# A decoder layer: attention scores from the turned raw residual times a centred Gram matrix of the context, the second norm folded into the epsilon of the scores' norm

## What is computed

```python
x = x + L0_attn_ref(layernorm(x), Wv, Wg, bg, Wq, bq, Wo)
x = x + L0_xattn_ref(layernorm(x), ctx_512, W_k, b_k, gamma, beta)
x = x + L0_ffn_ref(layernorm(x), router_w, gate_w, up_w, down_w, ...)

def L0_xattn_ref(p, k_v, W_k, b_k, ln_gamma, ln_beta):
    kv = k_v @ W_k.T + b_k
    out = einsum('bij,bjd->bid', p, kv)
    sim = einsum('bid,bjd->bij', out, kv) * 256 ** -0.5
    sim = (sim - mean(sim)) * rsqrt(var(sim) + 1e-6) * ln_gamma + ln_beta
    return softmax(sim)
```

## Time and profile before

| what | value |
|---|---|
| time, three runs | 166.57 us median (164.66 to 167.26) |
| span of the profiled execution, first to last instruction | 155.8 us |
| PE busy | 119.9 us (77%) |
| DVE busy | 108.1 us (69%) |
| POOL busy | 101.7 us (65%) |
| ACT busy | 69.8 us (45%) |
| DMA, mean over the span | 112 GB/s |

### The profile page before, as it was taken

One profiled execution on the slowest core, in us unless ns is written; L12 is line 12 of the kernel. 1 busy time (PEld: TensorE's weight loads), 2 busy tenths in 40 slices (PEclk: granted clock), 3 DMA queues, 4 the chain that ended last, 5 costly groups with the idle time before them and its releaser, 6 DMA issues. The chain is left out here.

```text
span 155.8 us, 2769 instructions
## 1 busy us (share of the span) xinstructions
PE 119.9 (77%) x709; PEld 97.2 (62%) x710; DVE 108.1 (69%) x303; ACT 69.8 (45%) x164; POOL 101.7 (65%) x145
## 2 busy tenths in 40 slices
PE   0199997997599658669879794459999979999700
PEld 0158986993387338347659594327878859888500
DVE  2672596949897999999699977122676866776510
ACT  3445878494396726794344401011434333343100
POOL 5346695696588828967858578605377776777540
PEclk9999999999999999975899999965999999999975
DMA  5997465236222251440222258283243334111000
GB/s 141 229 279 211 157 184 157 68 83 192 65 52 85 71 135 23 120 126 0 74 70 69 103 203 299 84 268 103 77 113 104 117 101 148 50 58 44 31 0 0
DMA packets 18206, 17.51 MB, mean 112 GB/s; under 512 B 4108, under 2 KB 17424, under 8 KB 18192
## 3 DMA queue, kind: packets, MB, share of 16 engines
q1 hardware_dynamic: 15792, 13.56, 30.8%
q0 software_dynamic: 1824, 3.22, 6.5%
q10 hardware_dynamic: 576, 0.56, 1.1%
HBM read 13.78 MB, written 5.38 MB: 123 GB/s over the span
## 5 line engine op out<-in xcount | busy, mean ns | idle before, releaser
L437 POOL TENSOR_TENSOR gu_lo<-stage,gu_hi 128x512 fp32r<-128x512 f32 x16 | 22.4, 1410 | 2.8 <-ACT gu_hi L502 2.8
L452 POOL DMA_INDIRECT tq<-base_rows,tid x15 | 15.4, 1026 | 13.1 <-DMA base_rows<-res 6.2
L457 POOL DMA_INDIRECT out_dram<-z,tid x15 | 15.2, 1012 | 7.6 <-DVE tid L851 2.6
L478 ACT ACTIVATE xn<-res,shift,rstd 128x256 f32<-128x256 f32 x22 | 12.0, 593 | 8.2 <-POOL shift L413 8.1
L405 POOL TENSOR_SCALAR vareps<-mv 128x2 f32<-128x2 f32 x16 | 4.2, 259 | 15.7 <-DVE mv L673 15.0
L409 POOL TENSOR_TENSOR rstd<-vareps,expo 128x2 f32<-128x2 f32 x16 | 12.4, 772 | 0.4
L1057 PE MATMUL bV<-shd,xn 128*128 128x256 f32 x32 | 9.6, 453 | 2.0 <-DVE xn L818 2.0
L670 DVE BATCH_NORM_STATS2 bn<-res 128x6 f32<-128x256 f32 x24 | 8.9, 413 | 3.0 <-DMA res<-in_x_dram 3.0
L437 POOL TENSOR_TENSOR dn_lo<-stage,dn_hi 128x512 fp32r<-128x512 f32 x8 | 11.0, 1371 | 0.0
L432 POOL DMA_INDIRECT x_sorted<-xs,dest x8 | 8.2, 1031 | 4.0 <-issue 2.6
L982 PE MATMUL bO<-wo,tq 128*128 128x256 f32 x32 | 7.8, 386 | 3.8 <-issue 2.8
(11 more groups left out here) (200 smaller groups left out, 386.4 us busy)
## 6 DMA issues: line engine op xcount, KB each, us to landing
stage<-in_L_ffn_gate_w_dram SPq DMA_DIRECT2D x8, 256.0 KB, 2.8
stage<-in_L_ffn_up_w_dram SPq DMA_DIRECT2D x8, 256.0 KB, 2.7
stage<-in_L_ffn_down_w_dram SPq DMA_DIRECT2D x8, 256.0 KB, 2.7
xs<-x_sorted SPq DMA_DIRECT2D x15, 136.0 KB, 2.2
res<-in_x_dram SPq DMA_DIRECT2D x4, 256.0 KB, 3.5
base_rows<-res SPq DMA_DIRECT2D x4, 256.0 KB
x_sorted<-pad SPq DMA_DIRECT2D x5, 136.0 KB, 3.4
x_sorted<-pad ACTq DMA_DIRECT2D x4, 136.0 KB, 3.3
```

The lines of the kernel that those rows point to most:

```text
L437: g.tensor_tensor(units[n][2], stage[:, n % RING], f32(units[n][1]), ALU.subtract).then_inc(unit_lo, 1)
L452: g.indirect_dma_start(rb[:, s % TILE_RING, :], None, base_rows, bass.IndirectOffsetOnAxis(tid[:, s:s + 1], 0), bounds_check=N - 1, oob_is ...
L457: g.indirect_dma_start(out_rows, bass.IndirectOffsetOnAxis(tid[:, s:s + 1], 0), ry[:, s % 2, :], None, bounds_check=N - 1, oob_is_err=Fals ...
L478: last = a.activation(dst[:, i, :], res[:, b * TB + i, :], ACT.Identity, bias=shift[:, kind, b, i:i + 1], scale=rstd[:, kind, b, i:i + 1])
```

## The change

- `norm2`, `rstd2` and their tile `xn2` are gone. PE turns the raw residual (`turn2` waits for `x2_made`).
- `turn_kv`, `context_mix` and `mixed` are gone. Instead the context is centred once: `kv_bias` now also sums each row (two instructions for each half, with an accumulator), and DVE subtracts the mean (`centre_kv:0`, `centre_kv:1`). PE makes one Gram matrix per batch from it (`gram:b`, 256 by 256), and ACT copies each out (`gram_copy:b`).
- `similarity` is the turned residual times the Gram matrix: four products with a full contraction, in place of two with 64 rows.
- `sim_stats` is gone from DVE: the rows are centred already, so ACT takes the mean square from `bS` (`sim_square`, two `Square` with an accumulator) and POOL adds `eps_row`, which is the second norm's variance times the scores' epsilon (`sim_eps`, one instruction in the place of `rstd2`).
- `sim_centre` multiplies by `rstd` and gamma and so waits for `sim_rstd`; `sim_scale` only adds beta.

```diff
 DVE_ORDER
-    stats1:0 weight_lo:0 norm1:0 weight_lo:1 stats1:1 weight_lo:2 turned1_lo:0 stats1:2 stats1:3
+    stats1:0 weight_lo:0 norm1:0 weight_lo:1 stats1:1 weight_lo:2 turned1_lo:0 centre_kv:0 centre_kv:1
...
 ACT_ORDER
-    weight_hi:10 turned_kv:0 weight_hi:11 norm2:0 gate_tanh:2 query_tanh:2 weight_hi:12 turned2:0
+    weight_hi:10 gram_copy:0 gram_copy:1 gram_copy:2 gram_copy:3 weight_hi:11 gate_tanh:2 query_tanh:2
...
 PE_ORDER
-    turn1:2 recall:0 value:1 turn_kv:0 gate:2 query:2 value:2 turn2:0 recall:1 context_mix:0 turn1:3
+    turn1:2 recall:0 value:1 gram:0 gram:1 gram:2 gram:3 gate:2 query:2 value:2 turn2:0 recall:1 turn1:3
...
+            def sim_eps(b):
+                pool.wait_ge(stats[LN2], b + 1)
+                g.tensor_scalar(eps_row[:, b, :], mv[:, LN2, b, :, 1], SIM_EPS / SIM_SCALE ** 2, LN_EPS * SIM_EPS / SIM_SCALE ** 2,
+                                ALU.mult, ALU.add).then_inc(eps_row_made, 1)
...
+                if kind == SIM:
+                    pool.wait_ge(eps_row_made, b + 1)
+                    g.tensor_tensor(vareps[:, kind, b, :], spread[:, b, :], eps_row[:, b, :], ALU.add).then_inc(eps_added[kind], 1)
...
-                a.activation(kvT_all[:, 2 * h:2 * h + 2, :], (psU, psM)[h][0:C], ACT.Identity,
-                             bias=bk[:, :]).then_inc(kvT_made[h], 1)
...
+                for i in range(2):
+                    last = a.activation(kvT(2 * h + i), (psU, psM)[h][0:C, i, :], ACT.Identity, bias=bk[:, :],
+                                        accum_out=kv_sum[:, 2 * h + i:2 * h + i + 1])
+                last.then_inc(kvT_made[h], 1)
+
+            def gram_copy(b):
+                act.wait_ge(gram_done, b + 1)
+                a.copy(gram_all[:, b], (psS, psU, psM, psS)[b]).then_inc(gram_made, 1)
+
+            def sim_square(b):
+                act.wait_ge(sm["sim_done"], b + 1)
+                if b >= 1:
+                    act.wait_ge(stats[SIM], b)
+                for i in range(TB):
+                    last = a.activation(junk[:, i, :], psS[:, i, :], ACT.Square, scale=SIM_SCALE, accum_out=spread[:, b, i:i + 1])
+                last.then_inc(stats[SIM], 1)
...
+            def centre_kv(h):
+                dve.wait_ge(kvT_made[h], 1)
+                v.tensor_scalar(kv_mean[:, 2 * h:2 * h + 2], kv_sum[:, 2 * h:2 * h + 2], 1.0 / S, None, ALU.mult).then_inc(kv_mean_made, 1)
+                dve.wait_ge(kv_mean_made, h + 1)
+                for c in (2 * h, 2 * h + 1):
+                    last = v.tensor_scalar(kvT(c), kvT(c), kv_mean[:, c:c + 1], None, ALU.subtract)
+                last.then_inc(kv_centred[h], 1)
...
-                dve.wait_ge(stats[SIM], b + 1)
-                for i in range(TB):
-                    last = v.scalar_tensor_tensor(z[:, i, :], psS[:, i, :], mv[:, SIM, b, i, 0:1], gam[:, :],
-                                                  ALU.subtract, ALU.mult)
+                dve.wait_ge(rstd_made[SIM], b + 1)
+                for i in range(TB):
+                    last = v.scalar_tensor_tensor(z[:, i, :], psS[:, i, :], rstd[:, SIM, b, i:i + 1], gam[:, :],
+                                                  ALU.mult, ALU.mult)
...
+            def gram(b):
+                pe.wait_ge(kv_centred[b // 2], 1)
...
+                if b == 3:
+                    pe.wait_ge(gram_made, 1)
+                for m in range(KT):
+                    last = T.matmul((psS, psU, psM, psS)[b][:, m, :], kvT(b)[:, m * P:(m + 1) * P], kvT(b), start=True, stop=True)
+                last.then_inc(gram_done, 1)
...
             def similarity(b):
+                pe.wait_ge(gram_made, B)
                 pe.wait_ge(sm["xT2_made"], b + 1)
...
                 for i in range(TB):
+                    for k in range(KT):
+                        last = T.matmul(psS[:, i, :], xT2[:, b % 2, k, i * P:(i + 1) * P], gram_all[:, b, k, :],
+                                        start=(k == 0), stop=(k == KT - 1))
```

More of the change, by code:

```diff
@@ L54 @@
[L54 to L57, removed]
+    weight_hi:10 gram_copy:0 gram_copy:1 gram_copy:2 gram_copy:3 weight_hi:11 gate_tanh:2 query_tanh:2
+    weight_hi:12 turned2:0 norm1:3 weight_hi:13 sim_square:0 turned1_hi:3 weight_hi:14 weight_hi:15
@@ L66 @@
-    sim_scale:3 route:1 residual3:3 turned3_lo:2 shared_hidden:1 route:2 shared_add:0 destination:1
-    turned3_lo:3 destination:2 shared_hidden:2 route:3 shared_add:1 destination:3 slot_table:3
-    shared_add:2 shared_hidden:3 shared_add:3
+    stats1:0 weight_lo:0 norm1:0 weight_lo:1 stats1:1 weight_lo:2 turned1_lo:0 centre_kv:0 centre_kv:1
+    stats1:2 stats1:3 turned1_lo:1 memory:0 turned1_lo:2 residual2:0 memory:1 memory:2 residual2:1
+    turned1_lo:3 sim_centre:0 sim_scale:0 residual2:2 residual3:0 sim_centre:1 memory:3 sim_scale:1
@@ L69 @@
+    turned3_lo:0 residual2:3 sim_centre:2 residual3:1 sim_scale:2 shared_hidden:0 route:0 residual3:2
+    destination:0 turned3_lo:1 sim_centre:3 sim_scale:3 route:1 residual3:3 turned3_lo:2 shared_hidden:1
+    route:2 shared_add:0 destination:1 turned3_lo:3 destination:2 shared_hidden:2 route:3 shared_add:1
+    destination:3 slot_table:3 shared_add:2 shared_hidden:3 shared_add:3
 """.split()
@@ L487, in norm1 @@
                 normalise(LN1, b, xn1[:, b % 2], "xn1_made")
[L489 to L492, removed]
             def norm3(b):
@@ L596, in shared_tanh @@
                 a.activation(hs[:, b % 2], psG, ACT.Tanh, scale=0.5).then_inc(sm["th_made"], 1)
-            steps = {"norm1": norm1, "norm2": norm2, "norm3": norm3, "weight_hi": weight_hi, "turned_wk": turned_wk, "turned_ctx": turned_ctx, "kv_bias": kv_bias,
-                     "turned_kv": turned_kv, "mixed": mixed, "turned1_hi": turned1_hi, "gate_tanh": gate_tanh,
+            steps = {"norm1": norm1, "norm3": norm3, "weight_hi": weight_hi, "turned_wk": turned_wk, "turned_ctx": turned_ctx, "kv_bias": kv_bias,
+                     "gram_copy": gram_copy, "sim_square": sim_square, "turned1_hi": turned1_hi, "gate_tanh": gate_tanh,
                      "query_tanh": query_tanh, "turned2": turned2, "softmax_exp": softmax_exp,
@@ L831, in _ @@
             steps = {"stats1": stats1, "norm1": norm1, "weight_lo": weight_lo, "turned1_lo": turned1_lo,
-                     "memory": memory, "residual2": residual2, "sim_stats": sim_stats,
+                     "memory": memory, "residual2": residual2, "centre_kv": centre_kv,
                      "sim_centre": sim_centre, "sim_scale": sim_scale, "residual3": residual3,
@@ L1061, in _ @@
             steps = {"turn1": turn1, "turn2": turn2, "turn3": turn3, "turn_wk": turn_wk, "turn_ctx": turn_ctx,
-                     "kv": kv, "turn_kv": turn_kv, "context_mix": context_mix, "recall": recall, "similarity": similarity,
+                     "kv": kv, "gram": gram, "recall": recall, "similarity": similarity,
                      "gate": lambda b: project(b, 0, psG, "g_done", "tg_made"),
```

108 lines of the change are left out of this document (43 added, 65 removed).

## The result

The change makes the kernel slower: 174.17 us median (172.97 to 175.10) against 165.62 (163.75 to 167.26), a ratio of 1.0545, 95% interval 1.0451 to 1.064. The prediction was 176.0 (170.5 to 181.0) with 0.84 on slower.

The account below looks back on a forecast made before the run. It took the chain through DVE to batch 3's scatter as the bound: 7.9 us late at `sim_centre:0` plus net 1.5 gives 9.4; span 155.8 becomes 165.2, with 10.8 outside 176.0 us (170.5 to 181).

Parts of the forecast that it names:

- The early wait: DVE stands still about 7 us for the context at `centre_kv:1`; `memory:0` starts at 24.8, 6.8 us late.
- From there to `gate:2`: Late weight subtractions, loads and copies on POOL, ACT and PE put `gate:2` at 37.0, 8.3 us late.
- the ring: Weight-load slots: `weight_lo:3` at 26.4 frees one late, the load lands at 30.5, and `weight_hi:7` waits for it.
- the half rate: Clock rival: PE, idle before `turned1_lo:1`, then runs at half rate, adding 2 to 3.4 us: 178 to 179.4; chance 0.21.
- The scores: Shorter chain from `memory:2` to the scores: `sim_centre:0` at 49.4 where it was 41.50, 7.9 us late.
- The waits for the root: `sim_centre` now waits for `rstd`: +2.7 us for batch 1, +1.5 for batch 3, 0 for batch 2.
- POOL's saving, put at nothing: POOL's four small instructions become one; this lies beside its waits, so it counts as nothing.
- The sum: Delay of 7.9 us at `sim_centre:0` plus net 1.5 from there to the scatter: 9.4 us slower.
- the wrong span: Profiled span of 155.8 us becomes 165.2, with 10.8 us taken to lie outside it.

Follow-up runs that it names:

- wait_alone: The kernel before with one wait added on DVE, for `kv_bias:1` ahead of the statistics of batch 2: 174.83 us, ratio 1.0395.
- late_centre: The changed kernel with both centring steps moved on DVE to behind `turned1_lo:2`: 169.48 us, ratio 1.0077 to the kernel before.
- ring_free: The changed kernel with POOL's first four weight subtractions moved ahead of `rstd1:2` and `rstd1:3`: 176.85 us, ratio 1.0527 to the kernel before.
- before_again: The kernel before, unedited, run again with a profile of its own: 168.21 us, ratio 1.0033.
- late_table_rstd: The changed kernel, centring behind `turned1_lo:2`, POOL's last three weight subtractions behind the slot table, `sim_rstd` ahead of `rstd3`: 165.26 us, ratio 0.9814 to before.
- before_table: The kernel before with POOL's last three weight subtractions behind DVE's slot table: 164.14 us, ratio 0.9769; run again, 163.62 us, 0.9946.

## Why the prediction was right

- **The early wait.** `kv_bias:1` done at 21.09 (forecast 21.4), the centring at 21.85 (22.3), `memory:0` at 24.15 (24.8): right, and wait_alone and late_centre show it as the main cause.
- **From there to `gate:2`.** The time was right (37.34 for 37.0) and the way wrong. The step that failed is the chain over POOL's `weight_lo:3`, the ring, `weight_hi:7` and `gram_copy:0`: each of its times came within 0.5 (26.87, 31.02, 31.55, 35.57), but ring_free takes it away and the time doesn't move. PE's own queue gave the same to within the 0.46 us that `gram:3` waited for `gram_copy:0`: `gate:1` at 24.49 behind DVE, 4.83 us to `turn1:2`, most of it at half rate (2.98 in before_again), 3.7 to the Gram products, 4.3 for these. The prediction gave PE full rate and left the half rate to a rival, as 2 to 3.4 on top. Its 1.9 us are in the 37.34, and 1.2 of them took the place of idle time that PE had ahead of `recall:0` in before_again. That two ways gave one time, so that `gate:2` came within 0.4 us, is luck.
- **The scores.** `sim_centre:0` at 49.11 (49.4): right.
- **The waits for the root.** The idle time ahead of `sim_centre:1` is 2.64 (2.7), ended by POOL. Ahead of `sim_centre:3` it is 0.75, where 1.5 was taken: this term was too large. And the first doesn't last: `sim_centre:2` comes 18.4 us behind `sim_centre:0` (18.7 in before_again). From `sim_centre:0` to the last scatter the change adds 0.2 us to before_again, not 1.5.
- **POOL's saving, put at nothing.** In the kernel before POOL was busy with `rstd2:0` while DVE ran the scans of `memory:1`, 1.27 us. With `sim_eps:0` in its place a weight subtraction runs there, and the scans last 2.30 in the changed kernel and 3.26 in late_table_rstd. That is a cost, hidden in the changed kernel by the 3.06 us that DVE waits for PE at `memory:2`. DVE and POOL before (`rstd2:0` is four instructions, 28.46 to 30.58), then with the change:

```profile
28.94 1.27 DVE L707 TENSOR_TENSOR_SCAN mem<-decay,tg 128x256 f32<-128x256 f32 x2
```

```profile
28.46 0.22 POOL L405 TENSOR_SCALAR vareps<-mv 128x2 f32<-128x2 f32 x1 [1.45 <-DVE mv L673]
```

```profile
34.96 2.30 DVE L714 TENSOR_TENSOR_SCAN mem<-decay,tg 128x256 f32<-128x256 f32 x2
```

```profile
35.10 1.60 POOL L445 TENSOR_TENSOR gu_lo<-stage,gu_hi 128x512 fp32r<-128x512 f32 x1
```

- **The sum.** 9.4 forecast, 8.55 between the medians, 7.8 between the last scatters of before_again and the changed kernel. Up to the scatter it was 1.6 too large, 1.3 of that in the stretch behind `sim_centre:0`. It also stood on the wrong span: 155.8 was a quick execution and 1.8 us lie outside the span. The sum came through since the quick part is all behind the last scatter, where nothing was counted, and that is luck too.

## What to carry to other kernels

A step that waits for something late must not be written ahead of work that is ready on an engine with a fixed order; moving two entries of a table gave back 4.7 of the 5.5 per cent. When the profiled span and the timed runs differ by several per cent, profile again before counting what lies outside the span. A chain that reproduces a time to 0.4 us isn't yet the cause: take its wait away and see whether the end moves. The same holds for a wait that an edit removes: look whether what follows stays sooner up to the last scatter.

## What the runs showed of the hardware

- DVE's instructions with two operands in SBUF took longer beside POOL's subtractions: 15 elements took 4.34 to 4.36 us in five profiles and 0.15 where POOL waited; the two scans of `memory:1` took 1.27 us beside POOL's small instructions and 3.26 beside a subtraction. The Trainium skill (SBUF — State Buffer, Summary: rules for kernel authors) says that an instruction with two SBUF inputs and a GpSimd instruction that reads SBUF get in each other's way, and that the one issued second blocks until the first has finished. The trace agrees that DVE was blocked, but here through three POOL instructions in a row, until the last had ended. Which was issued first it doesn't show: by the records of before_again DVE's began at 96.00, the first subtraction at 96.62.
- The two subtractions of the centring took 0.61 us, where twice 0.41 was counted.
- PE's first products (`gate:0`) took 0.63 us for a pair in some profiles and 0.40 in others of the same kernel (before_table: `gate:1` at 17.47 and, in its second run, 20.41). So single starts of two profiles compare only to some 3 us, unless they are counted from a point that both share.
- Every profile but the first of before has at least one pause of 3 to 4 us of POOL in the experts' loop; what makes them stayed open.
